# Graph attention with residual and layer norm on one core: six sort groups in place of five, and another order of the drain

## What is computed

```python
q = (x[src] @ qW).reshape(e, 4, 24)
k = (x[dst] @ kW).reshape(e, 4, 24)
v = (x[dst] @ vW).reshape(e, 4, 24)
s = exp(clip(sum(q * k, -1), -10, 10))            # (e, 4)
w = s / (segment_sum(s, src)[src] + 1e-8)
res = segment_sum(w[:, :, None] * v, src).reshape(n, 96)
y = x + (x + res)
out = (y - mean(y)) / sqrt(var(y) + 1e-5)         # over the 96 features
```

## Time and profile before

| | |
|---|---|
| timed executions, us | 1355.97, 1357.38, 1362.27 |
| the profiled execution: own time / span, us | 1364.9 / 1363.1 |
| busy: PE, DVE, ACT, POOL, us | 1050.7, 1019.2, 674.0, 957.1 |
| mean granted PE clock, share of full | 0.709 |
| HBM traffic over the span | 73 GB/s |
| instructions | 23400 |

### The profile page before, as it was taken

How to read it: one execution, slowest core, us unless ns; L and a number is a source line. 1 busy time by engine, 2 the same in 40 slices (tenths; PEclk the granted TensorE clock), 3 DMA queues, 4 the chain that set the end, 5 groups by cost and what they waited for, 6 DMA issues and landing times.

```text
span 1363.1 us, 23400 instructions
## 1 busy us (share of the span) xinstructions
PE 1050.7 (77%) x6502; PEld 935.0 (69%) x6503; DVE 1019.2 (75%) x2846; ACT 674.0 (49%) x1464; POOL 957.1 (70%) x911
## 2 busy tenths in 40 slices
PE   6896498776798786798887778887678888888850
PEld 4674497665787665698776667777577777777740
DVE  8797998689997678998758887777655555555556
ACT  4773299522599522399842225886232222222215
POOL 1203777777787777777777777777777777777745
PEclk9897599956699856599877555889665555555555
DMA  4300222222222222222222222222422222222212
GB/s 121 121 0 25 68 70 70 73 79 70 68 67 69 76 70 73 70 72 72 70 74 79 77 72 74 70 72 82 135 79 78 78 78 78 78 79 78 77 41 71
DMA packets 68298, 100.62 MB, mean 74 GB/s; under 512 B 33522, under 2 KB 53874, under 8 KB 68204
## 3 DMA queue, kind: packets, MB, share of 16 engines
q0 software_dynamic: 42240, 86.56, 23.3%
q1 hardware_dynamic: 25964, 12.94, 3.3%
HBM read 92.23 MB, written 7.22 MB: 73 GB/s over the span
## 4 chain that ended last, share of the span: by engine, by line
POOL 39%; DVE 18%; issue 16%; PE 14%; ACT 7%; DMA 4%; DVEq 2%; POOLq 0%; ACTq 0%; SPq 0%
POOL kv L466 39%; ACT steps_m L672 4%; PE ps_r L620 3%; DMA kv<-kv_table,dst_s 2%; DVE acc L1031 2%; PE ps_q L608 2%; DVE steps_m L800 2%; DVE prod L1039 2%; PE ps_a L594 1%; DVEq L392 1%; PE ps_b L594 1%; DMA acc<-in_x_dram 1%; DVE place_m L940 1%; DVE place_m L944 1%; ACT onehT L717 1%
## 5 line engine op out<-in xcount | busy, mean ns | idle before, releaser
L466 POOL DMA_INDIRECT kv<-kv_table,dst_s x880 | 921.9, 1048 | 329.5 <-issue 322.8
L620 PE MATMUL ps_r<-wv,oneh 128*128 128x100 f32 x1760 | 344.9, 366 | 127.4 <-DVE wv L1046 126.3
L620 PEld LDWEIGHTS ps_r<-wv,oneh 128*128 128x128 f32 x1760 | 312.5, 270 | 150.2 <-DVE wv L1046 141.1
L608 PE MATMUL ps_q<-qt,onehT 128*128 x1760 | 327.3, 353 | 90.9 <-ACT onehT L717 85.9
L608 PEld LDWEIGHTS ps_q<-qt,onehT 128*128 128x128 f32 x1760 | 298.3, 259 | 119.7 <-issue 118.6
L672 ACT ACTIVATE steps_m<-iota_f,pos_t 125x283 f16<-125x283 f32 (+4 forms) x778 | 321.3, 502 | 22.1 <-PE ps_b L594 13.9
L1031 DVE TENSOR_TENSOR acc<-acc,ps_r 128x100 f32 x880 | 223.2, 254 | 65.6 <-issue 32.4
L1039 DVE TENSOR_TENSOR prod<-ps_q,kv 128x480 f32<-128x480 f32 x176 | 115.3, 655 | 208.9 <-DMA kv<-kv_table,dst_s 201.2
L710 ACT ACTIVATE wv<-clipped 128x20 f32<-128x20 f32 x176 | 38.2, 217 | 433.1 <-DVE clipped L1073 432.9
L594 PE MATMUL ps_a<-steps_m,place_m 125*128 125x283 f16 (+4 forms) x778 | 197.8, 294 | 1.7 <-ACT steps_m L672 0.2
L717 ACT ACTIVATE onehT<-ps_t 128x640 f32<-128x640 bf16 x176 | 123.4, 701 | 148.6 <-PE ps_t L629 143.9
(11 more groups left out here) (185 smaller groups left out, 696.4 us busy)
## 6 DMA issues: line engine op xcount, KB each, us to landing
kv<-kv_table,dst_s POOLq DMA_INDIRECT x880
kv_table<-kv SPq DMA_DIRECT2D x7, 672.0 KB, 3.6
acc<-in_x_dram SPq DMA_DIRECT2D x6, 336.0 KB, 4.6
steps_m<-in_x_dram SPq DMA_DIRECT2D x6, 336.0 KB, 5.3
out_dram<-kv SPq DMA_DIRECT2D x6, 336.0 KB
src_i<-in_src_dram SPq DMA_DIRECT2D x1, 415.0 KB
dst_i<-in_dst_dram SPq DMA_DIRECT2D x1, 415.0 KB
acc<-in_x_dram SPq DMA_DIRECT2D x1, 288.0 KB, 5.7
```

The source lines that it names most:

```text
L466: nc.gpsimd.indirect_dma_start(kv[:, nm, u, :], None, kv_dram, bass.IndirectOffsetOnAxis(ap=dst_s[:, n * U + u:n * U + u + 1], axis=0)).th ...
L608: last = nc.tensor.matmul(ps_q[nm % 2][:, u * D:(u + 1) * D], onehT[:, nm % 2, u * P:(u + 1) * P], qt[:, bass.ds(blks[u], 1), :].rearrange ...
L620: last = nc.tensor.matmul(ps_r[nm % 2][:, u * RW:(u + 1) * RW], oneh[:, nm % 2, u, :], wv[:, nm % 2, u, :], start=True, stop=True)
```

## The change

The groups are now six, `GC = [120, 90, 110, 150, 180, 200]`, with widths of steps 166, 186, 205, 244, 274 and 293 elements, 13, 18, 21, 30, 35 and 59 iterations. The ranking of group g is spread over a computed number of passes (`ranked`: 5, 8, 8, 12 and 14), and the units of the sort over the passes that are left (9 units in 5 passes, 11 in 8, 15 in 10, 18 in 16, 20 in 19), so that a pass can carry two units. `differ` and `turn` stand behind one pass and `pick` behind the next. LS is 3 ahead of the second and third group and 4 ahead of the others.

In the prologue three wide constant arrays are made by ACT, eight small ones by POOL, the load of `src` is cut in two (first the 120 columns of the first group), x is loaded into four buffers in place of two, and `project` comes at other places of the list.

In the last passes DVE does weighing and additions ahead of the product, the last iteration's five sums go to five PSUM banks and are added one by one. In the drain POOL only multiplies by `den`, piece i behind the addition of piece i-1; DVE takes mean and variance of each block with one `bn_stats` and combines the two halves of its result (`total` adds 2x and makes the seven statistics of a piece, `spread_of` the variance by six small instructions, `scale_of` the reciprocal and the shift); ACT does the root once for each of four parts and normalises with scale and shift in one instruction; the last piece and three blocks of the one before are normalised by DVE.

```diff
-    LS = 4
+    LS = (3, 3, 4, 4, 4)
-    GC = [180, 150, 170, 190, 160]
+    GC = [120, 90, 110, 150, 180, 200]
...
-        project_after = {"mark0": (0,), "count": (1,), "base0": (2, 3), "sel0": (4,), "table": (5, 6)}
+        project_after = {"mark3": ("lift",), f"tally{len(ROUNDS[0]) - 1}": (0,), "count": (1,), "base1": (2,),
+                         "table": (3, 4, 5, 6)}
...
-            end = B0[g + 1] - LS
-            spare = end - 3 - (V0[g + 2] - V0[g + 1] + 1) - m
+            end = B0[g] - LS[g - 1]
+            count = end - m - 2
+            names = rank(g) + ["choose"]
+            units = V0[g + 1] - V0[g] + 1
+            ranked = round(count * (12 * GC[g] + 1000) / (34 * GC[g] + 1000))
+            at = shares(len(names), ranked)
+            for k in range(ranked):
                 m = plan_iters(m, 1)
-                to = len(names) * (k + 1) // spare
-                for name in names[at:to]:
-                    PLAN.append(("piece", name, g + 1))
-                at = to
-            m = plan_woven(m, g + 1)
-            for name in ("differ", "turn", "pick"):
-                m = plan_iters(m, 1)
-                PLAN.append(("piece", name, g + 1))
+                for name in names[at[k]:at[k + 1]]:
+                    PLAN.append(("piece", name, g))
+            at = shares(units, count - ranked)
+            PLAN.append(("iters", m, g, [tuple(range(V0[g] + a, V0[g] + b)) for a, b in zip(at, at[1:])]))
+            m = plan_iters(m + count - ranked, 1)
+            PLAN.append(("piece", "differ", g))
+            PLAN.append(("piece", "turn", g))
+            m = plan_iters(m, 1)
+            PLAN.append(("piece", "pick", g))
...
-            sp.dma_start(src_i[:, :], src.rearrange("(p c) -> p c", c=EC)).then_inc(s_src, 16)
+            sp.dma_start(src_i[:, 0:GC[0]], src_rows[:, 0:GC[0]]).then_inc(s_src[0], 16)
...
+            sp.dma_start(src_i[:, GC[0]:EC], src_rows[:, GC[0]:EC]).then_inc(s_src[1], 16)
...
+                pool.wait_ge(s_den, 1 if i == 0 else 2)
+                wait(pool, s_two, i)
+                y = acc[:, i * PC:(i + 1) * PC, 0:D].rearrange("p b (h d) -> p b h d", h=HEADS)
+                nc.gpsimd.tensor_tensor(y, y, den[:, i * PC:(i + 1) * PC, :].unsqueeze(3)
+                                        .to_broadcast([P, PC, HEADS, DH]), ALU.mult).then_inc(s_div, 1)
...
+                        final = isinstance(n, int) and n == NBT - 1
+                        to = ps_last[u][:, 0:RW] if final else ps_r[nm % 2][:, u * RW:(u + 1) * RW]
...
                 if sorts:
-                    unit(*sorts, halves=(1,))
+                    unit(*sorts[0], halves=(1,))
+                for sort in sorts[1:]:
+                    unit(*sort)
...
+                if isinstance(m, int) and m >= NBT - 1:
...
+                    weigh()
...
+                    for u in range(U):
+                        add_up(u)
+                    multiply()
+                    reduce()
+                    clip()
+                    return
...
+        PARTS = [(0, 1), (1, 3), (3, 5), (5, NPC)]
...
+            for j, (a, b) in enumerate(PARTS):
+                for i in range(a, b):
+                    total(i)
+                    if j and i == a:
+                        scale_of(j - 1)
+                spread_of(j)
+            scale_of(len(PARTS) - 1)
```

More of the change, by code:

```diff
@@ L631, in tiles @@
                     last.then_inc(s_ot, 1)
-                if sorts:
-                    unit(*sorts)
-            follow(pe, tiles, unit, {"project": project, "count": count, "table": table, "turn": turn, "pick": pick,
-                                     **{f"tally{r}": lambda g, r=r: tally(g, r) for r in range(len(ROUNDS[G - 1]))}})
+                for sort in sorts:
+                    unit(*sort)
+            follow(pe, tiles, unit, {"lift": transpose_x, "project": project, "count": count, "table": table, "turn": turn, "pick": pick,
+                                     **{f"tally{r}": lambda g, r=r: tally(g, r) for r in range(max(len(r) for r in ROUNDS))}})
         @block.scalar
         def _(act):
+            act.wait_ge(s_ramp, 1)
+            nc.scalar.activation(iota_s[:, :, :], iota_f[:, 0:P].unsqueeze(2).to_broadcast([P, P, SU]), ACT.Copy)
+            nc.scalar.activation(iota_d, iota_f[:, 0:T1].unsqueeze(2).to_broadcast([P, T1, KD]), ACT.Copy)
+            nc.scalar.activation(iota_t[:, :, :], iota_f[:, 1:P + 1].unsqueeze(2).to_broadcast([P, P, U]),
+                                 ACT.Copy).then_inc(s_wide, 1)
             def copy_xt(i):
@@ L705, in tiles @@
                 if sorts:
-                    unit(*sorts, halves=(0,))
+                    unit(*sorts[0], halves=(0,))
                 n, nm = m, mm
@@ new lines, in weigh @@
+                def weigh():
+                    n, nm = m - 1, (mm - 1) % R
+                    if there(n):
+                        dve.wait_ge(s_exp, n + 1)
+                        nc.vector.tensor_tensor(
+                            wv[:, nm % 2, :, 0:D].rearrange("p u (h d) -> p u h d", h=HEADS),
+                            kv[:, nm, :, D:2 * D].rearrange("p u (h d) -> p u h d", h=HEADS),
+                            wv[:, nm % 2, :, D:RW].unsqueeze(3).to_broadcast([P, U, HEADS, DH]),
+                            ALU.mult).then_inc(s_wv, 1)
@@ L1051, in tiles @@
+                if isinstance(m, int) and m == NBT - 2:
+                    coming[m - 1] = blocks_of(mybir.EngineType.DVE, m - 1)
+                multiply()
+                weigh()
                 if there(m - 2):
@@ new lines, in scale_of @@
+            def scale_of(j):
+                a, b = PARTS[j][0] * PC, PARTS[j][1] * PC
+                dve.wait_ge(s_std, j + 1)
+                link(nc.vector.reciprocal(inv[:, a:b], std[:, a:b]))
+                nc.vector.scalar_tensor_tensor(shift[:, a:b], both[:, a:b], -0.5, inv[:, a:b],
+                                               ALU.mult, ALU.mult).then_inc(s_inv, 1)
+            for j, (a, b) in enumerate(PARTS):
+                for i in range(a, b):
[3 more added lines that the diff above has]
+                spread_of(j)
@@ new lines, in _ @@
+            scale_of(len(PARTS) - 1)
+            dve.wait_ge(s_inv, len(PARTS))
+            for k in range(HALF, PC):
+                n = (NPC - 2) * PC + k
+                last = nc.vector.tensor_scalar(yout[NPC - 2][:, k, :], acc[:, n, 0:D], inv[:, n:n + 1],
+                                               shift[:, n:n + 1], ALU.mult, ALU.add)
+            last.then_inc(s_ylast, 1)
+            n = (NPC - 1) * PC
+            y = yout[NPC - 1]
+            link(nc.vector.tensor_tensor(y, acc[:, n:NB, 0:D], inv[:, n:NB].unsqueeze(2).to_broadcast([P, PC, D]),
+                                         ALU.mult))
@@ L1125 @@
+            nc.vector.tensor_tensor(y, y, shift[:, n:NB].unsqueeze(2).to_broadcast([P, PC, D]),
+                                    ALU.add).then_inc(s_ylast, 1)
 _INS = ['x', 'src', 'dst', 'L0_gnn_qW', 'L0_gnn_kW', 'L0_gnn_vW']
```

320 lines of the change are left out of this document (153 added, 167 removed).

## The result

The changed kernel takes 1369.34 us (median of five, 1367.07 to 1374.89) against 1357.85 for the kernel before on the same chip: a ratio of 1.0085 [1.0054, 1.0116], slower by 0.85%. The prediction said 1332.4 us, between 1312 and 1349. It was wrong, and on the other side of the kernel before. The profiled execution has a span of 1367.5 us.

The account below looks back on a forecast made before the run. POOL's back-to-back GpSimd fetches were taken to bound the kernel. Span 1363.1 - 33 (prologue) + 11 (stretch) + 10 (late picks) - 13 (drain) = 1338.1, giving a 1332.4 us median, range 1312 to 1349.

Parts of the forecast that it names:

- Late picks: +10 us: Between fetch groups: picks of the second to fourth group come late and POOL stalls; 15 by the sum, 10 taken.
- the sort is late by 20 to 30: Rival: DVE's work is 3 to 4% more than assumed, so picks come later; 1341 to 1352 us, chance 0.18.
- PE can't carry two units: Rival: in two-unit passes PE's clock stays at 1.2 GHz, 12 to 13 us a pass; 1363 us, chance 0.07.
- The sort keeps up: Rival: no pick is late beside the fetches; 1312 to 1322 us, chance 0.20.
- the drain gains nothing: Rival: after the last fetch, statistics or the POOL/DVE alternation take as long as what went; 1345 us, chance 0.05.
- Prologue: -33 us: Before the first fetch: 12 sort units in place of 18 and an earlier lead-up; first fetch at 88, between -26 and -38.
- Stretch: +11 us: Fetches beside sorting: 73 units at 0.81 us and five rankings at 6.4 lengthen them, 91.1 us against 79.7.
- Drain: -13 us: From the last fetch to the end: work moved ahead, statistics beside multiplications; 39 us against 52, between -16 and -6.

Follow-up runs that it names:

- one unit a pass: Changed kernel's own groups, LS 3, 3, 4, 4, 4, with Y = 8 and ranked = max(4, count - units): 1351.44 us, 0.9957.
- Y = 8: Changed kernel with a fetch waiting for PE's iteration n-8 in place of n-6: 1374.19 us, 1.0104.
- wider arrays: Changed kernel with ACT's arrays of steps 293 elements wide in units of all groups but the first, added columns unused: 1390.5 us, 1.024.
- the best run: Changed kernel with groups 140, 110, 120, 140, 160, 180, LS 4, ranked = max(4, count - units), Y = 8, `pay` behind the pairs, HALF = 1: 1326.07 us, 0.9763.
- the roomy kernel with one unit a pass: Changed kernel with groups 160, 120, 130, 150, 150, 140, LS 4, ranked = max(4, count - units): 1338.55 us, 0.9861.

## Why the prediction was wrong

**Late picks: +10 us.** This is the step that failed. The mechanism was named, with its three places, but its size was 50, not 10: 33 at the picks and 17.5 inside the groups. Working from the prediction's numbers: for the second to fourth group it set 397 us of DVE's, ACT's and PE's work against 382 of POOL's, 15 late, of which it took 10. Measured were 406.7 against 355.1, 51.6 late. 10 of the missing us are on the sort's side: the ends of the three picks, taken at 17 each, were 20.9, 20.6 and 22.8, because ACT and PE are still behind when DVE comes to `differ`, and the rest of the sort took 3.6 us less than it had been given, though a two-unit pass of the fourth group took 10.0 where 9.6 was taken. 27 are on POOL's side, which the prediction thought slower than it is: it charged the three groups 47.5 us of stretch (35 units and three rankings) and 4 us of slow first fetches. The windows show 70.64 + 95.11 + 111.30 - 260 x 0.957 = 28.2. Those are 23 of the 27; the other 4 are in its sums, for with its own terms the 130 and 153 us of the third and fourth group come out 2 to 3 us lower each. Part of the smaller stretch follows from the stalls, as a late fetch has less sorting beside it: with one unit a pass, where POOL hardly waits, the same windows have 36.5. The errors of both sides fell into a difference of two numbers near 390, which is small against either. The last 5 are the choice of 10 rather than 15 "since the ends of the groups overlap", which no row supported; they don't overlap, as the holes show. The prediction gave its own condition: 31 us late if DVE's work is 4% more. The sort's side was 2.4% more, and POOL's 7% less. That POOL's side could be too high was not among its rivals.

The packing was in the sum, pass by pass: 9.6 + 3.55 = 13.2 us for a pass with two units and a plain one, against 2 x 5.5 = 11 for one unit in each. But it wasn't named as a cost of its own, and at these sizes it is the larger part of the stalls: spread over the passes, the same groups stall 36.5 us less.

Behind the size stands a choice of view. The prediction read that the last pick had 12.3 us in hand and called this what the change spends. Slack is not a stock: it is the difference of two rates, and with 13 iterations beside a sort of 90 columns in place of 25 beside 150, one rate changes by itself.

**The rival "the sort is late by 20 to 30"** was the right mechanism at half its size. **"PE can't carry two units"** ended at the measured side (1363), but its condition, a clock that stays at the lower level, didn't hold: the granted clock in those passes was 0.88 (the prediction had 1.00), a two-unit pass took 10.0 us and not 12 to 13, ACT was nearly full in them, and ACT's extra work came through to the time. What the missing 0.12 of the clock cost wasn't measured. **"The sort keeps up"** fell with the holes, and **"the drain gains nothing"** with the 11 us of the drain.

**Prologue: -33 us.** -29. The sort's rate was right (33.9 us for 12 units, 33.6 predicted), as was the way from its end to the first fetch. The lead-up was too hopeful: first matmul at 51.2, not 47.5. The earlier start met the load of `dst`, 4.8 us of wait that the prediction didn't have. Putting `pay` behind the pairs takes most of it away and brought the first fetch 2.6 and 4.0 us forward on the two chips that ran both. The number itself varies: the three runs with the same prologue (Y = 8, one unit a pass, wider arrays) have the first matmul at 48.6, 49.1 and 53.1 and the first fetch at 90.2, 90.6 and 93.5. 92.3 lies below the 95 that the prediction named as its limit.

**Stretch: +11 us.** The fetches' own time is 5.7 us shorter. In the run where the same groups hardly stall it is 9.2 longer than before, near the 11. So the sum of parts was about right, and the stalls took it away again: a fetch that is late has less sorting beside it. For a unit the 0.81 us is borne out from another side: three tensor_tensor at 0.23 make 0.69. The 6.4 for a ranking looks too much: in the best run 916.8 - 880 x 0.957 - 71 x 0.81 leaves 17, 3.4 for each of five; in the roomy kernel with one unit a pass it is 4.5, in the change's groups with that rule 6.0.

**Drain: -13 us.** -11. 10.3 us ahead of the first multiplication where 8.7 was said. The weighing and additions that moved in front of the product aren't quite hidden there: DVE is idle 2.2 us ahead of the weighing, and the last product starts 3.3 us behind the end of the last fetch (1329.71 against 1326.45) where it was 1.7 before (1312.73 against 1311.06). That is the 1.6 us. The statistics took 1.22 us (1.2). ACT's scaling with a shift takes 5.12 / 14 = 0.366 us a block where the scaling alone took 3.80 / 14 = 0.27; the last root stands behind it, and DVE's reciprocal waits 2.3 us for that root. No second table load appeared.

**The sum** with the measured terms: 1363.1 - 29 - 6 + 50 - 11 = 1367, the span. The prologue was off by 4 us, the stretch by -17, the drain by 2, the late picks by 40: 29 us together, and 1338.1 + 29 is the span. The other 7.5 us between the forecast of 1332.4 and the measured 1369.3 are the step from the profiled execution down to the median, which the prediction took from the kernel before; the changed kernel's profiled execution was its median.

## What to carry to other kernels

When work for the next batch is hidden beside the current one, write both sides for the smallest batch, each from rows of that batch's kind: how long the batch lasts alone, and how long the next one's preparation takes with its waits at the end. A margin of 2 us in 116 was enough, and a deficit of 13 in 90 cost 13 us at the first late pick, so start from the first batch that just carries the next (140 columns here, in place of 120) and grow the later ones; and spread the preparation evenly over the passes rather than in pairs, since what a batch can carry depends on it. Where the preparation is what is late, letting the fetches run further ahead only moves the wait. Leave some margin: the best plan here was the worst on another chip.

## What the runs showed of the hardware

- A DVE tensor_tensor with two f16 operands in SBUF, 125x1280 and 0.81 us long, adds about 0.2 us to the issue of indirect DMAs on GpSimd (15.8 us for 69 in one comparison, 13.0 on another chip); fetches that overlap with such arrays take 1.354 us, the others 0.985.
- Seven `bn_stats` of 96 elements take 1.22 us, 0.17 each, where one DVE addition over the same 672 takes 0.84.
- An activation of 128x96 with a scale and a shift from SBUF (Identity) takes 0.366 us, with the scale alone (Copy) 0.27.
- There is a chip on which the same kernel takes 1570 us instead of 1358, with waits of up to 22 us put down to "remote", and on which a plan that gains 2.4% elsewhere loses 5.7%.
